# A two-stage attention kernel: the MLP of the first stage computed by rows with folded weights, started inside the attention loop

## Chip, cores and metric

The kernel runs on one core of one Trainium2 chip. The metric is the device time in microseconds (us) of one execution; the median over several executions is compared. Engines are named TensorE (PE in the rows), VectorE (DVE), ScalarE (ACT), GpSimd (POOL) and SyncE (SP).

## The reference

Four images of 16 x 16 pixels and 128 channels pass two layers. Cut to what matters here:

```
# layer 0: attention with 8 heads over 64 sampled points, residual, MLP, residual
x_ln = layernorm(x, ln_g, ln_b)
q = x_ln @ wq + bq                 # -> depthwise conv, gelu, offsets -> sampled keys and values
att = softmax(qh @ kh.T) @ vh      # 8 heads of 16 channels
z = att @ mo_w + mo_b + x
out = gelu(layernorm(z, ln_g, ln_b) @ mlp_w + mlp_b) + z          # called x1 below
# layer 1: group norm (32 groups, over pixels and 4 channels), full attention, residual
xg = groupnorm(x1) * gn_gamma + gn_beta
q, k, v = xg @ wq + bq, xg @ wk + bk, xg @ wv + bv
y = softmax(q @ k.T / sqrt(C)) @ v @ wo + bo + x1
```

## The kernel before

Everything stays on chip after the loads. Each engine has its own program, written out by hand, with semaphores between them; nothing schedules it. Where an instruction waits, all that stands behind it on its engine waits too. "bank" is one of eight PSUM banks of 512 fp32 columns; only TensorE writes them, and VectorE and ScalarE read them. GpSimd reads and writes SBUF only.

The stages:
- Until about 24 us: loads, layer norm of x, convolution, sampling, keys of the first two images.
- The loop of the first attention (lines 1048 to 1063 of TensorE's program), over T = 8 tiles of 128 pixels (two per image). Step i transposes the shifted scores of tile i (transpose_scores), multiplies with the values for tile i-1 (value_tile), projects tile i-2 (out_project), makes the scores of tile i+2 (score_tile) and transposes the normalised result of tile i-1 (att_transpose). VectorE takes maxima, subtracts, normalises and adds the residual (z_tile), ScalarE takes exponentials and copies. At i = 2, fold_second (line 914) makes the folded weight w_vo = wv wo and three bias columns in bank 7; ScalarE's fold_out (line 411) copies them out.
- The bridge, from the loop to the second attention. Per image b: bn_stats and bn_aggr of z (z_stats, z_aggr), the variance plus eps (z_var), its power -1/2 on GpSimd (z_scale, line 314), z_hat = (z - mean) * rstd on VectorE (zhat_image, line 648), transposes of z and z_hat to channels x pixels (z_transpose, line 1002), ScalarE's copy of the latter into z_t (zt_image), one matmul of 256 columns with mlp_wg = ln_g * mlp_w (mlp_image, line 1020), Gelu with a bias column (gelu_image), and the sum with the transposed z (x1_image, line 653) in transposed layout x1_t. gelu_transpose turns gel_t back to rows for the residual of layer 1, which VectorE adds to z_res (x1_residual, line 658); z_res = z + out_bias comes from GpSimd (residual, line 319). The output bias in out_bias is made by three matmuls after z_transpose(0) (lines 1174 to 1178).
- Group norm in two sets of two images: gn_stats, gn_aggr; gn_mean (line 1071) multiplies the means with a matrix that leaves each channel's deviation from its group; gn_square (line 700) squares it on VectorE, gn_spread (line 1083) sums the variances, gn_var adds eps, gn_pow on GpSimd takes the power -1/2, and norm_image (line 712) writes x_gn. keep_warm (line 812) issues bf16 matmuls on a bank nobody reads; three pairs stand in the bridge (lines 1190 to 1196).
- The second attention, from gn_mean(1) at line 1208: project_qk, project_v, score_image, transposes and value products per image, and finish_tile (line 731), which writes y with the residual x1_res.

VectorE's order in the bridge stands in lines 746 to 805, ScalarE's in lines 448 to 476, GpSimd's in lines 332 to 345, TensorE's in lines 1172 to 1228.

Of the kernel before, what the change touches and what calls it, by code (L numbers as in the profile page):

```python
# [37 lines left out]
def reach(shift, n):  # L38
# [10 lines left out]
              ("mk_b", 1), ("mv_b", 1), ("gn_gamma", 1), ("gn_beta", 1), ("bq1", 1), ("bk1", 1), ("bv1", 1), ("mlp_b", 1),  # L49
# [3 lines left out]
    "late": [("mlp_w", C), ("wv1T", C), ("wo1", C), ("wq1", C), ("wk1", C), ("group_mean", P), ("group_rest", P)],  # L53
}
ROWS = ["bq_conv", "ln_b", "mo_b", "bo1"]
# [13 lines left out]
def build(nc, x, early, fold, mid, late, rows, ln_rows, out):  # L69
    ctx = ExitStack()  # L70
    with ctx:
# [27 lines left out]
        def r(name):  # L99
# [17 lines left out]
        cols1 = sb("cols1", [P, 3])  # L117
# [3 lines left out]
        mlp_wg = sb("mlp_wg", [P, C])  # L121
        msa_bias = sb("msa_bias", [P, C])
# [30 lines left out]
        z_hat = sb("z_hat", [P, T, C])  # L153
        z_t = sb("z_t", [P, T, P])
        gel_t = sb("gel_t", [P, B, HW])
# [26 lines left out]
                fold1_mm w_vo_ok cols1_ok outbias_mm outbias_ok msabias_mm msabias_ok mlpw_ok gamma_ok""",  # L182
# [4 lines left out]
            "norm of z and MLP": "zst_ok zmv_ok zve_ok zrs_ok zhat_ok zt_mm zt_ok mlp_mm gel_ok zres_ok x1t_ok gelt_mm x1res_ok",  # L187
# [80 lines left out]
        def _(pool):  # L268
# [50 lines left out]
            def residual(b):  # L319

                pool.wait_ge(s["z_ok"], 2 * b + 2)
                pool.wait_ge(s["outbias_ok"], 1)
                pool.tensor_tensor(z_res[:, 2 * b:2 * b + 2, :], z[:, 2 * b:2 * b + 2, :],
                                   out_bias[:, :].unsqueeze(1).to_broadcast([P, S, C]), ALU.add).then_inc(s["zres_ok"], 1)
# [10 lines left out]
            pool.wait_ge(s["w_vo_ok"], 1)  # L335
            pool.tensor_scalar(w_vog[:, :], w_vo[:, :], w("gn_gamma"), None, ALU.mult).then_inc(s["gamma_ok"], 1)
            z_scale(1)
            residual(0)
            residual(1)
# [3 lines left out]
            residual(2)  # L343
            residual(3)
            gn_pow(1)

        @block.scalar
        def _(act):
# [61 lines left out]

            def fold_out():
                act.wait_ge(s["fold1_mm"], 1)
                act.copy(w_vo[:, :], bank[7][:, 0:C]).then_inc(s["w_vo_ok"], 1)
                for j, name in enumerate(("bq1", "bk1", "mlp_b")):
                    act.activation(cols1[:, j:j + 1], bank[7][:, C + j:C + j + 1], ACT.Identity, bias=w(name)).then_inc(s["cols1_ok"], 1)
# [28 lines left out]
            def gelu_image(b):  # L444
                act.wait_ge(s["mlp_mm"], b + 1)
                act.activation(gel_t[:, b], bank[3 + b][:, 0:HW], ACT.Gelu, bias=cols1[:, 2:3]).then_inc(s["gel_ok"], 1)

            for i in range(T - 1):
# [61 lines left out]
        def _(dve):  # L510
# [156 lines left out]
            for i in range(T - 1):  # L667
# [21 lines left out]
                if i >= 5 and i % 2 == 1:  # L689
                    zhat_image((i - 5) // 2)  # L690
# [602 lines left out]
```

## Time and profile before

| | us |
|---|---|
| median of 3 runs | 79.36 (79.25 to 79.98) |
| the profiled execution's own time | 79.27 |
| its span in the trace | 77.40 |
| TensorE matmuls busy | 70.6 (91% of the span) |
| VectorE busy | 51.7 (67%) |
| ScalarE busy | 33.9 (44%) |
| GpSimd busy | 24.3 (31%) |

The span is what the trace shows from the first to the last instruction; the 1.87 us around it are start and end of the execution. A row of a timeline gives start, duration, engine, line and operation, then output<-inputs, the shapes and how many instructions are merged ("x2"). In square brackets stands the idle time of the engine before the row and who ended it. An fp32 matmul is recorded as two instructions, a transpose as one. A matmul's duration includes its latency: in a row of several, the next starts long before the last has ended, so the time that one takes from the queue is read from start to start.

### The profile page before, as it was taken

To read this page: it belongs to the slowest core of one execution; us is meant where nothing else is said; L and a number is where in the kernel's file an instruction comes from. 1 tells how busy PE (TensorE), PEld (TensorE's weight loads), DVE (VectorE), ACT (ScalarE), POOL (GpSimd) and SP (SyncE) were. 2 spreads that over 40 slices of the span, in tenths; PEclk is the share of its full clock that TensorE was granted. 3 is DMA by queue.
4 is the path that set the end of the run, shared out by engine and by line. 5 is a ranking of instruction groups with operands and counts; after the bars stand their busy time and mean duration, and the time that the engine had idled before them with its cause. 6 is when DMAs were issued, how large, how long until landed. Compare 5 with 4: busy or idle time off the path is not lost.

```text
span 77.4 us, 1968 instructions
## 1 busy us (share of the span) xinstructions
PE 70.6 (91%) x732; PEld 53.6 (69%) x732; DVE 51.7 (67%) x172; ACT 33.9 (44%) x84; POOL 24.3 (31%) x37
## 2 busy tenths in 40 slices
PE   4999699998999999999999999998897999998950
PEld 2345599783786647879777989845485869996830
DVE  0478742116366959477789968599799786868480
ACT  6112397068139563524424419820248048263600
POOL 5008999900000038390019137123820030000000
PEclk9999999999999999999999999999999999999999
DMA  0789870000000000000000000000000000010112
GB/s 9 226 270 150 305 289 12 0 8 0 0 8 0 0 0 4 0 0 8 0 0 0 4 0 0 8 0 0 0 0 0 0 0 4 0 68 9 59 55 89
DMA packets 3051, 3.07 MB, mean 40 GB/s; under 512 B 225, under 2 KB 2657, under 8 KB 3042
## 3 DMA queue, kind: packets, MB, share of 16 engines
q1 hardware_dynamic: 3042, 2.95, 12.8%
q8 instruction: 6, 0.10, 0.5%
q14 instruction: 3, 0.02, 0.1%
HBM read 2.42 MB, written 0.52 MB: 38 GB/s over the span
## 4 chain that ended last, share of the span: by engine, by line
PE 63%; DVE 17%; issue 5%; DMA 5%; ACT 3%; SPq 2%; POOL 2%; DVEq 0%; POOLq 0%; ACTq 0%
PE bank L810 53%; DMA x_hw<-x 5%; PE bank L971 5%; PE bank L1140 2%; DVE smax L604 2%; DVE x_t L656 1%; DVE gst L694 1%; SPq L247 1%; DVE st L528 1%; DVE bilin L578 1%; DVE x_gn L716 1%; DVE dist_y L562 1%; PE bank L989 1%; DVE q_conv L517 1%; POOL grs L330 1%
## 5 line engine op out<-in xcount | busy, mean ns | idle before, releaser
L810 PE MATMUL bank<-k_blk,qh 128*128 128x512 f32 x16 | 8.4, 605 | 0.0
L810 PE MATMUL bank<-v_blk,p_t 128*128 128x34 f32 x64 | 7.8, 267 | 0.0
L810 PEld LDWEIGHTS bank<-v_blk,p_t 128*128 128x128 f32 x64 | 7.8, 192 | 0.0
L810 PE MATMUL bank<-warm 128*128 128x512 bf16 x18 | 6.3, 471 | 1.0 <-POOL warm L269 1.0
L604 DVE TENSOR_REDUCE smax<-bank 128x8 f32<-128x512 f32 x8 | 5.5, 685 | 2.4 <-PE bank L810 2.4
L317 POOL TENSOR_TENSOR zrs<-zve,neg_half 128x2 f32<-128x2 f32 x4 | 2.9, 714 | 12.7 <-DVE zve L646 12.7
L810 PE MATMUL bank<-q_ph,wd 128*32 128x112 f32 (+5 forms) x256 | 6.8, 249 | 0.0
L303 POOL TENSOR_TENSOR x_res<-x_st,msa_bias 128x1024 f32<-128x1024 f32 x1 | 2.4, 2358 | 12.8 <-DVE bilin L578 12.8
L431 ACT ACTIVATE p_t<-bank 128x512 f32<-128x512 f32 x8 | 4.8, 597 | 3.4 <-PE bank L971 3.4
L810 PEld LDWEIGHTS bank<-q_ph,wd 128*32 128x32 f32 x256 | 5.6, 109 | 0.7 <-issue 0.3
L611 DVE TENSOR_TENSOR s_sub<-bank,smax 128x512 f32<-128x512 f32 x8 | 5.5, 682 | 0.1
L280 POOL TENSOR_TENSOR wd<-pack_early 128x512 f32<-128x512 f32 x4 | 4.1, 1046 | 4.4 <-DVE x_hat L540 4.4
L810 PE MATMUL bank<-v,p_t 128*128 128x129 f32 x32 | 4.8, 284 | 0.6 <-ACT p_t L233 0.4
L810 PEld LDWEIGHTS bank<-v,p_t 128*128 128x128 f32 x32 | 4.2, 190 | 1.2 <-issue 1.0
L971 PE MATMUL bank<-pack_early,s_sub 128*128 128x128 f32 x32 | 5.0, 279 | 0.0
L488 ACT ACTIVATE p<-bank,nmax 128x256 f32<-128x256 f32 x8 | 3.4, 476 | 3.0 <-DVE nmax L728 2.8
L438 ACT COPY att_t<-bank 128x128 f32<-128x128 f32 x8 | 2.1, 263 | 5.4 <-PE bank L989 5.3
L971 PEld LDWEIGHTS bank<-pack_early,s_sub 128*128 128x128 f32 x32 | 3.7, 144 | 0.8 <-issue 0.5
L810 PE MATMUL bank<-k,q 128*128 128x256 f32 x16 | 4.2, 385 | 0.0
L528 DVE BATCH_NORM_STATS2 st<-x_hw 128x6 f32<-128x128 f32 x8 | 1.8, 283 | 3.2 <-DMA x_hw<-x 3.2
L810 PEld LDWEIGHTS bank<-warm 128*128 128x128 bf16 x18 | 2.0, 122 | 2.9 <-issue 1.9
L810 PE MATMUL bank<-pack_mid,att_t 128*128 128x128 f32 x16 | 3.7, 311 | 0.2 <-DVE z L634 0.2
(149 smaller groups left out, 161.2 us busy)
## 6 DMA issues: line engine op xcount, KB each, us to landing
x_st<-x SPq DMA_DIRECT2D x1, 512.0 KB, 6.7
pack_late<-late SPq DMA_DIRECT2D x1, 448.0 KB, 7.3
out<-y SPq DMA_DIRECT2D x3, 128.0 KB, 1.7
pack_fold<-fold SPq DMA_DIRECT2D x1, 320.0 KB, 4.1
pack_mid<-mid SPq DMA_DIRECT2D x1, 261.0 KB, 5.8
x_hw<-x SPq DMA_DIRECT2D x2, 128.0 KB, 2.2
x_hw<-x SPq DMA_DIRECT2D x1, 256.0 KB, 3.8
pack_early<-early SPq DMA_DIRECT2D x1, 184.0 KB, 2.5
```

What stands on the lines that cost most here:

```text
L280: pool.tensor_tensor(wd[:, n:n + WD_CHUNK].rearrange("p n k j -> p (n k) j"), w("ident32").unsqueeze(1).to_broadcast([P, WD_CHUNK * PHASES ...
L303: pool.tensor_tensor(x_res[:, :, :], x_st[:, :, :].rearrange("p b (s c) -> p (b s) c", s=S), msa_bias[:, :].unsqueeze(1).to_broadcast([P, ...
L317: pool.tensor_tensor(zrs[:, 2 * b:2 * b + 2], zve[:, 2 * b:2 * b + 2], neg_half[:, 0:2], ALU.pow).then_inc(s["zrs_ok"], 1)
L431: act.activation(p_t[:, i % 2].rearrange("p j q -> p (j q)"), bank[5 + i % 2][:, :], ACT.Exp).then_inc(s["exp_ok"], 1)
L438: act.copy(att_t[:, i % 2], bank[0][:, 0:P]).then_inc(s["attt_ok"], 1)
L488: act.activation(p1[:, b % 2, t], bank[5 + b % 2][:, t * HW:(t + 1) * HW], ACT.Exp, bias=nmax1[:, 2 * b + t:2 * b + t + 1]).then_inc(s["p1 ...
L528: dve.bn_stats(st[:, i], x_hw[:, i]).then_inc(s["stats"], 1)
L604: dve.tensor_reduce(smax[:, i % 2], scores(i), AX.X, ALU.max).then_inc(s["smax_ok"], 1)
L611: dve.tensor_tensor(s_sub[:, i % 2], scores(i), smax[:, i % 2].unsqueeze(2).to_broadcast([P, NH, PIX]), ALU.subtract).then_inc(s["ssub_ok" ...
L810: return pe.matmul(o, l, r_, start=start, stop=stop, **k)
L971: m = pe.transpose(bank[5 + i % 2][:, j * P:(j + 1) * P], s_sub[:, i % 2, 2 * j:2 * j + 2].rearrange("p h q -> p (h q)"), w("ident"))
L1140: m = pe.transpose(bank[(2, 0)[t]][:, j * P:(j + 1) * P], p1[:, b % 2, t, j * P:(j + 1) * P], w("ident"))
```

## The change

1. The mean is taken out of the MLP's weights. A new constant center = I - 1/128 is loaded (in the pack "late"), and fold_mlp multiplies it with mlp_wg: z @ (center mlp_wg) is (z - mean) @ mlp_wg. The same function makes ln_b @ mlp_w + mlp_b as a full 128 x 128 block of equal rows. ScalarE copies both to mlp_wc (mlp_out).
2. The MLP works on rows: mlp_image multiplies z_t (now the transpose of z itself) as the stationary operand with mlp_wc, two matmuls of 128 columns into the upper half of zt_bank(b). VectorE's scaled_image multiplies with rstd and adds the bias block (u, two instructions per image); ScalarE's Gelu reads u from SBUF without a bias; gelu_transpose transposes gel into zt_bank(b), and x1_image adds z_t to it. z_hat, its transposes and zhat_image are gone.
3. x1_res = gel + z_res is added on GpSimd inside residual; x1_residual is gone from VectorE. GpSimd does residual(0) after the x_gn of images 0 and 1, and residual(1) to residual(3) after the last x_gn, behind gn_pow(1). The product w_vog moves behind gn_pow(0).
4. At i = 2 of the loop fold_mlp stands where fold_second stood. z_transpose(0) and zt_image(0) move into the loop (i = 5). mlp_image(0) and z_transpose(1) come right behind the loop. fold_second and the output bias (output_bias) move behind out_project(7) and mlp_image(3), into bank 6.
5. gn_square(0) runs on ScalarE as one Square; gn_square(1) stays on VectorE.
6. The three pairs of warm-up matmuls in the bridge are gone. Bank and semaphore waits follow the new places.

The diff, cut to its core:

```diff
-    "late": [("mlp_w", C), ("wv1T", C), ("wo1", C), ("wq1", C), ("wk1", C), ("group_mean", P), ("group_rest", P)],
+    "late": [("mlp_w", C), ("wv1T", C), ("wo1", C), ("wq1", C), ("wk1", C), ("group_mean", P), ("group_rest", P), ("center", P)],
...
 def residual(b):
+    t = slice(2 * b, 2 * b + 2)
     pool.wait_ge(s["z_ok"], 2 * b + 2)
     pool.wait_ge(s["outbias_ok"], 1)
...
+    pool.wait_ge(s["zres_ok"], b + 1)
+    pool.wait_ge(s["gel_ok"], b + 1)
+    pool.tensor_tensor(x1_res[:, t], gel[:, t], z_res[:, t], ALU.add).then_inc(s["x1res_ok"], 1)
...
             z_scale(1)
-            residual(0)
-            residual(1)
             z_scale(2)
             z_scale(3)
             gn_pow(0)
-            residual(2)
-            residual(3)
+            pool.wait_ge(s["w_vo_ok"], 1)
+            pool.tensor_scalar(w_vog[:, :], w_vo[:, :], w("gn_gamma"), None, ALU.mult).then_inc(s["gamma_ok"], 1)
+
+            pool.wait_ge(s["xgn_ok"], 2)
+            residual(0)
             gn_pow(1)
+
+            pool.wait_ge(s["xgn_ok"], B)
+            for b in range(1, B):
+                residual(b)
...
+            def mlp_out():
+                act.wait_ge(s["foldm_mm"], 1)
+                act.copy(mlp_wc[:, :], bank[7][:, 0:2 * C]).then_inc(s["mlpf_ok"], 1)
...
             def gelu_image(b):
-                act.wait_ge(s["mlp_mm"], b + 1)
-                act.activation(gel_t[:, b], bank[3 + b][:, 0:HW], ACT.Gelu, bias=cols1[:, 2:3]).then_inc(s["gel_ok"], 1)
+                t = slice(2 * b, 2 * b + 2)
+                act.wait_ge(s["u_ok"], 2 * b + 2)
+                act.activation(gel[:, t], u[:, t], ACT.Gelu).then_inc(s["gel_ok"], 1)
...
             att_tile(T - 1)
-            zt_image(2)
+            gn_square(0)
             gelu_image(2)
+            fold_out()
             zt_image(3)
+            act.wait_ge(s["outbias_mm"], 1)
+            act.copy(out_bias[:, :], bank[6][:, HW:HW + C]).then_inc(s["outbias_ok"], 1)
             gelu_image(3)
...
-            def zhat_image(b):
+            def scaled_image(b):
+                dve.wait_ge(s["mlp_mm"], b + 1)
                 dve.wait_ge(s["zrs_ok"], b + 1)
-                for i in (2 * b, 2 * b + 1):
-                    dve.tensor_scalar(z_hat[:, i], z[:, i], zmv[:, i, 0:1], zrs[:, i:i + 1], ALU.subtract, ALU.mult).then_inc(s["zhat_ok"], 1)
+                dve.wait_ge(s["mlpf_ok"], 1)
+                for t in range(S):
+                    i = 2 * b + t
+                    dve.scalar_tensor_tensor(out=u[:, i], in0=zt_bank(b)[:, HW + t * C:HW + (t + 1) * C], scalar=zrs[:, i:i + 1], in1=mlp_wc[:, C:2 * C],
+                                             op0=ALU.mult, op1=ALU.add).then_inc(s["u_ok"], 1)
...
-                dve.wait_ge(s["gel_ok"], b + 1)
-                dve.tensor_tensor(x1_t[:, b], gel_t[:, b], zt_bank(b)[:, HW:2 * HW], ALU.add).then_inc(s["x1t_ok"], 1)
...
                 dve.wait_ge(s["gelt_mm"], b + 1)
-                dve.wait_ge(s["zres_ok"], b + 1)
-                dve.tensor_tensor(x1_res[:, 2 * b:2 * b + 2], bank[3 + b][:, HW:2 * HW].rearrange("p (s c) -> p s c", s=S),
-                                  z_res[:, 2 * b:2 * b + 2], ALU.add).then_inc(s["x1res_ok"], 1)
+                dve.tensor_tensor(x1_t[:, b], zt_bank(b)[:, 0:HW], z_t[:, 2 * b:2 * b + 2, :].rearrange("c s q -> c (s q)"), ALU.add).then_inc(s["x1t_ok"], 1)
...
+            def fold_mlp():
+
+                pe.wait_ge(s["mlpw_ok"], 1)
+                pe.wait_ge(s["qh_ok"], 2)
+                mm(bank[7][:, 0:C], w("center"), mlp_wg[:, :])
+                mm(bank[7][:, C:2 * C], w("ln_b").to_broadcast([P, P]), w("mlp_w"), stop=False)
+                mm(bank[7][:, C:2 * C], ones_row[:, :], r("mlp_b"), start=False).then_inc(s["foldm_mm"], 1)
...
+            def output_bias():
+                pe.wait_ge(s["w_vo_ok"], 1)
+                pe.wait_ge(s["cols1_ok"], 2)
+                o = bank[6][:, HW:HW + C]
+                mm(o, w("bv1").to_broadcast([P, P]), w("wo1"), stop=False)
+                mm(o, w("gn_beta").to_broadcast([P, P]), w_vo[:, :], start=False, stop=False)
+                mm(o, ones_row[:, :], r("bo1"), start=False).then_inc(s["outbias_mm"], 1)
...
                 if i == 2:
-                    fold_second()
+                    fold_mlp()
+                if i == T - 3:
+                    z_transpose(0)
+
+            mlp_image(0)
+            z_transpose(1)
```

VectorE's queue around the group norm of images 0 and 1 stood before as follows (gve and gmean are the statistics of gn_var, x_res is x1_res, x_t is x1_t):

```order
L709 TENSOR_SCALAR gve<-bank 128x2 [waits gvar_mm]
L710 COPY gmean<-bank 128x2
L651 TENSOR_SCALAR z_hat<-z,zmv,zrs 128x128 [waits zrs_ok]
L651 TENSOR_SCALAR z_hat<-z,zmv,zrs 128x128
L716 TENSOR_SCALAR x_gn<-x_t,gmean,grs 128x256 [waits grs_ok,gmean_ok] x2
L661 TENSOR_TENSOR x_res<-bank,z_res 128x256 [waits zres_ok,gelt_mm]
L656 TENSOR_TENSOR x_t<-gel_t,bank 128x256 [waits gel_ok]
L694 BN_STATS gst<-x_t 128x6 [waits x1t_ok]
L722 TENSOR_SCALAR q<-bank,cols 128x256 [waits cols1_ok,qk_mm]
L723 TENSOR_SCALAR k<-bank,cols 128x256
```

And now (u is the scaled MLP output of image 3, x_t that of image 2):

```order
L725 TENSOR_SCALAR gve<-bank 128x2 [waits gvar_mm]
L726 COPY gmean<-bank 128x2
L679 TENSOR_TENSOR x_t<-bank,z_t 128x256 [waits gelt_mm]
L709 BN_STATS gst<-x_t 128x6 [waits x1t_ok]
L673 SCALAR_TENSOR_TENSOR u<-bank,zrs,mlp_wc 128x128 [waits mlpf_ok,zrs_ok,mlp_mm]
L673 SCALAR_TENSOR_TENSOR u<-bank,zrs,mlp_wc 128x128
L732 TENSOR_SCALAR x_gn<-x_t,gmean,grs 128x256 [waits grs_ok,gmean_ok] x2
L738 TENSOR_SCALAR q<-bank,cols 128x256 [waits cols1_ok,qk_mm]
L739 TENSOR_SCALAR k<-bank,cols 128x256
```

The x1 of image 2, its statistics and the two scaled rows of image 3 stand ahead of the x_gn pair, where two z_hat stood; x1 of image 2 waits for gelt_mm, a transpose by TensorE.

TensorE's queue from the group norm's second step to the first projection stood before as follows:

```order
L810 MATMUL bank<-gmv,pack_late 128x2 [waits dev2_ok]
L810 MATMUL bank<-dev,pack_late 128x2
L810 MATMUL bank<-gmv,pack_late 128x2
L1014 MATMUL bank<-pack_early,z 128x128 [waits x1t_ok,z_ok]
L1014 MATMUL bank<-pack_early,z 128x128
L1017 MATMUL bank<-pack_early,z_hat 128x128 [waits zhat_ok]
L1017 MATMUL bank<-pack_early,z_hat 128x128
L1014 MATMUL bank<-pack_early,z 128x128 [waits x1t_ok,z_ok]
L1014 MATMUL bank<-pack_early,z 128x128
L1017 MATMUL bank<-pack_early,z_hat 128x128 [waits zhat_ok]
L1017 MATMUL bank<-pack_early,z_hat 128x128
L810 MATMUL bank<-z_t,mlp_wg 128x256 [waits att_ok,mlpw_ok,zt_ok]
L810 MATMUL bank<-x_gn,wq1g 128x256 [waits x1res_ok,gamma_ok,xgn_ok]
L810 MATMUL bank<-x_gn,wk1g 128x256
```

And now, with the output bias (rows with w_vo and row) inside:

```order
L821 MATMUL bank<-gmv,pack_late 128x2 [waits dev2_ok]
L821 MATMUL bank<-dev,pack_late 128x2
L821 MATMUL bank<-gmv,pack_late 128x2
L821 MATMUL bank<-mlp_wc,z_t 128x128 [waits mlpf_ok,zt_ok]
L821 MATMUL bank<-mlp_wc,z_t 128x128
L821 MATMUL bank<-pack_late,pack_early 128x128 [waits cols1_ok,w_vo_ok]
L821 MATMUL bank<-w_vo,pack_early 128x128
L821 MATMUL bank<-row,ones_row 128x128
L1093 MATMUL bank<-pack_early,gel 128x128 [waits u_ok,gel_ok]
L1093 MATMUL bank<-pack_early,gel 128x128
L821 MATMUL bank<-x_gn,wq1g 128x256 [waits ssub_ok,gamma_ok,xgn_ok]
L821 MATMUL bank<-x_gn,wk1g 128x256
```

The transpose of gel of image 2 that x1 waits for now stands behind the MLP of image 3 and the output bias, and ahead of the projection.

ScalarE's queue ahead of the copy that the MLP of image 3 needs (the second z_t below; the cols rows are the two bias columns of layer 1) stood before:

```order
L438 COPY att_t<-bank 128x128 [waits msa_mm,attt_mm]
L442 COPY z_t<-bank 128x256 [waits zt_mm]
L446 ACTIVATE gel_t<-bank,cols 128x256 [waits mlp_mm]
L442 COPY z_t<-bank 128x256 [waits zt_mm]
L446 ACTIVATE gel_t<-bank,cols 128x256 [waits mlp_mm]
```

And now:

```order
L453 COPY z_t<-bank 128x256 [waits zt_mm]
L449 COPY att_t<-bank 128x128 [waits msa_mm,attt_mm]
L463 ACTIVATE dev<-bank 128x2 [waits dev_mm]
L458 ACTIVATE gel<-u 128x256 [waits u_ok]
L424 COPY w_vo<-bank 128x128 [waits fold1_mm]
L426 ACTIVATE cols<-bank,pack_early 128x1 x2
L453 COPY z_t<-bank 128x256 [waits zt_mm]
```

The square, the Gelu of image 2 and the copies of w_vo and two columns stand between the two z_t copies now.

## Rows read from the trace of the kernel before

**Rows 1.** TensorE's timeline, loop of the first attention and just behind it: start, duration, instruction.
```profile
34.53 0.39 PE L810 MATMUL bank<-pack_late 128*128 128x128 f32 x2
...
35.34 0.63 PE L971 MATMUL bank<-pack_early,s_sub 128*128 128x128 f32 x4
...
42.94 0.60 PE L971 MATMUL bank<-pack_early,s_sub 128*128 128x128 f32 x4
...
44.49 0.38 PE L1014 MATMUL bank<-pack_early,z 128*128 128x128 f32 x2
44.71 0.38 PE L1017 MATMUL bank<-pack_early,z_hat 128*128 128x128 f32 x2
44.93 0.39 PE L810 MATMUL bank<-pack_late,pack_early 128*128 128x128 f32 x2
...
45.89 0.66 PE L971 MATMUL bank<-pack_early,s_sub 128*128 128x128 f32 x4
```

**Rows 2.** TensorE's timeline, 52 to 61 us.
```profile
52.32 0.38 PE L810 MATMUL bank<-gmv,pack_late 128*128 128x2 f32 x2
...
56.15 0.70 PE L810 MATMUL bank<-x_gn,wq1g 128*128 128x256 f32 x2 [0.26 <-DVE x_gn L716]
...
57.12 0.59 PE L810 MATMUL bank<-z_t,mlp_wg 128*128 128x256 f32 x2
57.55 0.38 PE L1068 MATMUL bank<-pack_early,gel_t 128*128 128x128 f32 x2
...
60.12 0.38 PE L810 MATMUL bank<-gmv,pack_late 128*128 128x2 f32 x2 [0.54 <-DVE gmv L698]
```

**Rows 3.** VectorE's timeline, 49 to 67 us.
```profile
49.40 0.29 DVE L626 TENSOR_TENSOR att<-bank,recip 128x128 f32<-128x128 f32 x1
...
50.30 0.42 DVE L656 TENSOR_TENSOR x_t<-gel_t,bank 128x256 f32<-128x256 f32 x1 [0.32 <-ACT gel_t L446]
...
52.02 0.24 DVE L698 BATCH_NORM_AGGREGATE gmv<-gst 128x2 f32<-128x6 f32 x2
...
55.36 1.46 DVE L716 TENSOR_SCALAR x_gn<-x_t,gmean,grs 128x256 f32<-128x256 f32 x2 [0.40 <-POOL grs L330]
...
57.87 0.47 DVE L722 TENSOR_SCALAR q<-bank,cols 128x256 f32<-128x256 f32 x1
...
58.97 0.41 DVE L656 TENSOR_TENSOR x_t<-gel_t,bank 128x256 f32<-128x256 f32 x1
...
59.76 0.30 DVE L698 BATCH_NORM_AGGREGATE gmv<-gst 128x2 f32<-128x6 f32 x2
...
63.12 0.73 DVE L716 TENSOR_SCALAR x_gn<-x_t,gmean,grs 128x256 f32<-128x256 f32 x2 [0.22 <-POOL grs L330]
...
66.33 0.35 DVE L738 SCALAR_TENSOR_TENSOR y<-bank,rec,x_res 128x128 f32<-128x128 f32 x1
```

**Rows 4.** GpSimd's timeline, 34 to 57 us.
```profile
34.14 0.61 POOL L312 TENSOR_SCALAR mlp_wg<-pack_late,pack_early 128x128 f32<-128x128 f32 x1
...
54.47 0.79 POOL L330 TENSOR_TENSOR grs<-gve,neg_half 128x2 f32<-128x2 f32 x1 [0.61 <-DVE gve L709]
55.22 1.45 POOL L323 TENSOR_TENSOR z_res<-z,out_bias 128x256 f32<-128x256 f32 x2
```

**Rows 5.** ScalarE's timeline, 36 to 55 us.
```profile
36.65 0.58 ACT L415 ACTIVATE cols<-bank,pack_early 128x1 f32<-128x1 f32 x3
...
47.63 1.28 ACT L466 ACT_TABLE_LOAD   x1
...
49.80 0.85 ACT L446 ACTIVATE gel_t<-bank,cols 128x256 f32<-128x256 f32 x2 [0.23 <-PE bank L810]
...
54.72 0.37 ACT L442 COPY z_t<-bank 128x256 f32<-128x256 f32 x1 [3.92 <-PE bank L1017]
```

**Rows 6.** The page, part 2: granted clock of TensorE in 40 equal slices, in tenths.
```profile
PEclk9999999999999999999999999999999999999999
```

**Rows 7.** The chain that ended last, in order of time: start, duration, work.
```profile
64.26 3.07 PE bank L810 x20
```

More of the change, by code:

```diff
@@ L186, in build @@
             "attention": """s_mm smax_ok ssub_ok pt_mm exp_ok av_mm recip_ok att_ok attt_mm attt_ok msa_mm xres_ok z_ok""",
-            "norm of z and MLP": "zst_ok zmv_ok zve_ok zrs_ok zhat_ok zt_mm zt_ok mlp_mm gel_ok zres_ok x1t_ok gelt_mm x1res_ok",
+            "norm of z and MLP": "zst_ok zmv_ok zve_ok zrs_ok zt_mm zt_ok mlp_mm u_ok gel_ok zres_ok gelt_mm x1t_ok x1res_ok",
             "group norm": "gst_ok gmv_ok dev_mm dev2_ok gvar_mm gve_ok gmean_ok grs_ok xgn_ok",
@@ L786, in _ @@
             gn_aggr(3)
-            x1_residual(3)
             gn_square(1)
@@ L1013, in z_transpose @@
                 for t in range(S):
-                    pe.transpose(zt_bank(b)[:, HW + t * P:HW + (t + 1) * P], z[:, 2 * b + t], w("ident"))
-                pe.wait_ge(s["zhat_ok"], 2 * b + 2)
-                for t in range(S):
-                    m = pe.transpose(zt_bank(b)[:, t * P:(t + 1) * P], z_hat[:, 2 * b + t], w("ident"))
+                    m = pe.transpose(zt_bank(b)[:, t * P:(t + 1) * P], z[:, 2 * b + t], w("ident"))
                 m.then_inc(s["zt_mm"], 1)
@@ L1021, in mlp_image @@
                 pe.wait_ge(s["zt_ok"], b + 1)
-                pe.wait_ge(s["mlpw_ok"], 1)
-                if b < 2:
-                    pe.wait_ge(s["ssub_ok"], T - 1 + b)
-                else:
-                    pe.wait_ge(s["att_ok"], T)
-                mm(bank[3 + b][:, 0:HW], mlp_wg[:, :], z_t[:, 2 * b:2 * b + 2, :].rearrange("c s q -> c (s q)")).then_inc(s["mlp_mm"], 1)
+                pe.wait_ge(s["mlpf_ok"], 1)
+                for t in range(S):
+                    m = mm(zt_bank(b)[:, HW + t * C:HW + (t + 1) * C], z_t[:, 2 * b + t], mlp_wc[:, 0:C])
+                m.then_inc(s["mlp_mm"], 1)
             N = len(SHIFTS)
@@ L1181, in _ @@
             value_tile(T - 2)
+            mlp_image(1)
             out_project(T - 3)
-            z_transpose(1)
             value_tile(T - 1)
             att_transpose(T - 2)
-            mlp_image(0)
-            mlp_image(1)
-            out_project(T - 2)
-            att_transpose(T - 1)
-            keep_warm(2, 6)
-            out_project(T - 1)
             gelu_transpose(0)
             gelu_transpose(1)
-            keep_warm(2, 6)
+            out_project(T - 2)
+            z_transpose(2)
+            att_transpose(T - 1)
+            mlp_image(2)
+            out_project(T - 1)
+            fold_second()
             gn_mean(0)
-            keep_warm(2, 6)
+            z_transpose(3)
             gn_spread(0)
-            z_transpose(2)
-            z_transpose(3)
-            mlp_image(2)
+            mlp_image(3)
+            output_bias()
+            gelu_transpose(2)
             project_qk(0)
-            mlp_image(3)
-            gelu_transpose(2)
+            gelu_transpose(3)
             project_v(0)
-            gelu_transpose(3)
             project_qk(1)
```

109 lines of the change are left out of this document (51 added, 58 removed).

## The prediction, made before the changed kernel had run

> **What bounds the kernel now.** I read the chain of waits first, then the timelines of the four engines between 34 and 64 us, because every edit lies there. Three stretches matter. In the loop of the first attention TensorE never waits: its rows follow each other without idle time from the folded weights at 34.53 to the last out-projection of the loop, whose successor starts at 44.49 [rows 1]. From there to 60.12 the kernel hops between engines (transpose, copy, Gelu, transpose, add, statistics, group norm), and what counts is the order in which each queue meets its waits. TensorE's idle time before 60.12 (0.54 us, released by VectorE's gmv) shows where this bridge ends [rows 2]. From 60.12 on, the second attention runs mostly on TensorE, and the change leaves its order as it was. So I take the start of gn_mean(1), 60.12, as the marker: what moves it moves the end. Readers should see in the rows of VectorE that from 55.36 to 60.06 that engine has almost no idle time [rows 3], while around 50 to 55 it shares the path with GpSimd and ScalarE.
>
> **The start and the loop.** The DMAs change by some columns: center adds 64 KB to a pack that GpSimd needs only at 34.14 [rows 4]. I count nothing.
> fold_mlp takes fold_second's place in TensorE's queue, but it reads mlp_wg, which GpSimd finishes at 34.14 + 0.61 = 34.75 [rows 4], while fold_second started at 34.53 [rows 1]. A wait costs some 0.06 more (gmv ends at 59.76 + 0.30 = 60.06, TensorE starts at 60.12 [rows 2, 3]), so the fold starts at 34.81: +0.28. Queued behind it are the score transposes of every later tile. The old fold took 35.34 - 34.53 = 0.81. The new one is three matmuls like those of the output bias before, 45.89 - 44.93 = 0.96 [rows 1]: +0.15. As TensorE does not wait until 44.49, all of this persists. The two transposes of z, now inside the loop, add 44.71 - 44.49 = 0.22 [rows 1]. The loop ends at 44.49 + 0.28 + 0.15 + 0.22 = 45.14.
> After the loop four transposes and the output bias go (1.40 us up to 45.89). One MLP (57.55 - 57.12 = 0.43 [rows 2]) and two transposes (0.22) come: 45.79. So tile 7 is transposed 0.1 earlier than before; the second MLP costs its 0.43 a little later.
>
> **What is gained by 52 us.** ScalarE copies z_t of image 0 in the loop and no longer ahead of the table load. The load starts one copy (0.37) and a little earlier, near 47.2 (now 47.63), and takes 1.28; the Gelus run from about 48.55 to 49.4 (now from 49.80) [rows 5]. Transposing gel back takes 0.11 of pitch and 0.27 of latency, so the first comes back near 49.5. VectorE first normalises attention tile 7, now at 49.40 [rows 3]: ahead of that tile's matmuls an MLP of 0.43 has replaced four transposes of 0.44, and a statistic and an aggregate more stand ahead of its reciprocal on VectorE, so I take 49.54 for it, and 0.21 later, at 49.75 instead of 50.30, x1 of image 0 starts. It ends at 50.16, and gmv, with one z addition fewer on the way, ends near 51.6 instead of 52.02 + 0.24 = 52.26 [rows 3]. The six warm-up matmuls go; they filled waits, so they give nothing.
>
> **Where it is lost again.** gn_mean(0) stands behind z_transpose(2), mlp_image(2), out_project(7) and fold_second. z_transpose(2) waits for the first x1 (50.16, so it starts at 50.22): transposes land at 50.66, ScalarE's copy (0.37 [rows 5]) at 51.06, the MLP takes 0.50 (0.43 running, and some 0.07 for the start after a wait: two of 256 columns take 0.97 from 56.15), the out-projection 0.3 (three matmuls of that size take 0.96 [rows 1]), the fold about 0.22 + 2 x 0.20 = 0.62 (0.81 less one column of the old fold's three): gn_mean(0) starts at 52.55, and now at 52.32 [rows 2]. The 0.68 won on VectorE is thus gone. Squaring on ScalarE (0.20 from the matmul's end at 52.90, as three one-column activations take 0.58) instead of two VectorE operations, and then the same matmuls and the same power on GpSimd, gives the scale near 55.0 (now 54.47 + 0.79 = 55.26) [rows 4].
> But VectorE is not there to use it: between gn_var(0) and norm_image(0) now stand x1 of image 2, its statistics and scaled_image(3). x1 of image 2 waits for a transpose which TensorE issues behind mlp_image(3) and output_bias, and mlp_image(3) waits for ScalarE, where the fourth z_t copy stands behind square, Gelu 2, the w_vo copy and two bias columns. In numbers: 53.04 after the square, + 0.38 Gelu (two take 0.85), + 0.16 for the w_vo copy (bounds 0 and the 0.37 of a copy twice as wide; I take the middle), + 2 x 0.19 for the columns (three take 0.58), + 0.37 for the copy: 54.33 [rows 5]. TensorE: 54.39, mlp_image(3) 0.50, output_bias 0.96, two transposes 0.38 to their end: 56.23. VectorE: x1 and statistics 59.76 - 58.97 = 0.79, then two scaled rows. These read PSUM and SBUF as the y operation does, which takes 0.35; less 0.08 of overlap each, 0.54. Their bounds are 0.35 a piece and 0.21, half of the 0.42 that an addition of twice the columns takes; I take the row of the same form. x_gn starts at 57.6, instead of 55.36.
> Here the largest gain of the change is paid out: residual additions on GpSimd waited for x_gn. Now the pair x_gn takes 1.46 while GpSimd adds z_res (55.22, 1.45 long), and 0.73 at 63.12, where GpSimd is idle [rows 3, 4]. After the change GpSimd waits until the pair is done. The first x_gn ends at 58.0 and TensorE projects at 58.06, against 56.15: +1.91.
>
> **What is won back.** The projection ends 0.97 + 0.16 later, 59.19, so q1 starts at 59.2 against 57.87 (VectorE was busy with a residual, x1 and statistics until then): +1.33. The residual between k1 and x1 of image 3 is gone (1.10 from q1 to x1 now, 0.78 after): x1 starts at 59.98 against 58.97. Statistics and gmv follow as before, and gn_mean(1) starts near 61.1 against 60.12: +0.97 [rows 2, 3].
> The second attention then starts from the same state. GpSimd's residuals of images 1 to 3, 1.45 each after the last x_gn (63.85 + 0.97), end near 66.3, 67.7 and 69.2, before the y rows of their images need them (the first of all is at 66.33 now, and image 0 is ready early). They cost nothing; gn_pow(1) stands before them.
> The sum is 79.27 us (the profiled execution; its span is 77.40) + 0.97 = 80.24. It lies 0.09 below the median of the runs shown, 79.36, for the same kernel. I predict 80.2.
> One term can be read otherwise. The new Gelu has neither bias column nor PSUM source; the nearest row has both, two in 0.85, which is 0.38 to the next start and 0.47 for one [rows 5], and the sum uses that.
> The Trainium skill (ScalarE: Activation LUTs, What ACT_TABLE_LOAD costs) gives 186 ns + 0.833 ns per column without such a column operand, 0.40 for 256. By it one Gelu on the path is 0.07 shorter and the time would be 80.17. No row here shows that form of Gelu.
>
> **Rivals.**
> *The clock falls (82.0).* TensorE loses its warm-up matmuls and gets a hole of 2 us at 56 to 58, beside some 2 us of smaller waits from 49 on. Against it: the granted clock is 9 tenths or more in every slice of the profile now, those of the start included [rows 6]. For it: the longest wait of TensorE in this stretch is 0.54 us now [rows 2]. If the clock goes to 1.2 GHz, matmuls take double: a stretch such as 64.26 to 67.33, 3.07 us of TensorE [rows 7], would take 3 more; with part hidden by waits I price 1 to 3 over my sum: 81.2 to 83.2.
> The Trainium skill (TensorE: Matmul & The Clock Gate, What's actually happening) says that the slow clock is the default and activity releases it. By that rule a quiet bridge can be punished after it, not in it; the trace, at full clock throughout, neither shows nor excludes it.
> *The loop has cover (79.5).* If the fold's wait and longer matmuls are absorbed (VectorE or ScalarE late anyway in that iteration) and the ScalarE queue before the fourth copy is shorter, 0.43 and 0.2 to 0.3 go from the sum.
> *VectorE is released early (faster, 77.8 to 78.5).* One condition decides: the transpose of gel of image 2 must land by 53.7, so that x1, statistics and the scaled rows (0.79 + 0.54) lie under the wait for the rsqrt. Then x_gn starts at 55.0, its pair costs 0.73 instead of 1.46, q1 starts at 56.6, and gn_mean(1) near 58.6: -1.5. By my sum the transpose lands at 56.23, 2.5 us too late. Half of the way would give about no change.
> *GpSimd blocks VectorE in the second attention (80.9).* If operations from PSUM suffer as x_gn did, one projection output behind each of the additions from 64.8 to 69.2 loses up to 0.7. Against it: a projection output reads PSUM, while x_gn reads SBUF alone; no row shows one beside GpSimd.
>
> **How the numbers follow.** My sum 55% (79.8 to 80.6 by its term sizes); loop covered 17%; clock 11%; released or half released 12%; GpSimd blocking 5%. The range 79.0 to 81.6 leaves out the released case and the upper clock case. More than 1% (0.8 us, about what a measurement of this kernel can tell from no change) slower means over 80.15: slightly over half of my case, the clock, the blocking: 0.50. Faster 0.11. Within 1%: 0.39.
>
> **What would show it.** Right: TensorE's first fold row at about 34.8; x1 of image 0 near 49.8; VectorE idle for nearly 2 us after gmean, released by TensorE; x_gn as a pair of 0.73; a TensorE hole of 2 us before the projection; 61.1 for gn_mean(1). Wrong: x_gn starting before 56, a granted clock below 9 anywhere, or VectorE rows longer than now between 64 and 69 us.

## The result and the profile after

The changed kernel takes 81.94 us (81.47 to 83.04, 4 executions), the kernel before 79.31 beside it: ratio 1.029 [1.024, 1.035]. The forecast was 80.2, with a range of 79.0 to 81.6. The direction is right, the size is not: the rival "the clock falls" is what happens in most executions. The mean granted clock of TensorE was 1.000 in the execution of 81.47, and 0.974, 0.956 and 0.958 in those of 81.66, 82.23 and 83.04. Ratios here and below compare only the executions of each kernel that lie within 1.5% of its fastest; medians and ranges are of all of them.

Two things have to be taken apart before the profiles can be compared. First the start. The profiled execution of after (81.47, its span 79.7) ran late before any changed work. TensorE's timeline of after:

```profile
4.70 0.59 PE L821 MATMUL bank<-pack_early,ones_col 128*1 128x128 f32 x2
5.22 1.03 PE L821 MATMUL bank<-warm 128*128 128x512 bf16 x2
6.04 1.05 PE L821 MATMUL bank<-pack_early,x_hat 128*128 128x128 f32 x6
```

and of before:

```profile
4.68 0.60 PE L810 MATMUL bank<-warm 128*128 128x512 bf16 x2
5.21 1.00 PE L810 MATMUL bank<-pack_early,x_hat 128*128 128x128 f32 x6
```

Two warm-up matmuls take 1.03 instead of 0.60: full speed comes later here. In the clock records of the traces it sets in 6.48 us after the start in after and 3.81 in before (the page shows 9 for the time ahead of it too). The first score transpose starts at 27.73 instead of 26.65: 1.08 late. That differs from execution to execution: over the traces below it starts at 26.61 to 27.27 in kernels made from before, at 26.31 to 27.73 in those made from after. The two ranges overlap, so the late start is not put down to the change. I take 1.08 off every time of after below ("net").

Second the bridge. TensorE's timeline of after, from the fold in the loop to gn_mean(1):

```profile
35.87 0.49 PE L821 MATMUL bank<-mlp_wg,pack_late 128*128 128x128 f32 x2
...
36.93 0.66 PE L997 MATMUL bank<-pack_early,s_sub 128*128 128x128 f32 x4
...
46.78 0.38 PE L1040 MATMUL bank<-pack_early,z 128*128 128x128 f32 x2
47.17 0.63 PE L997 MATMUL bank<-pack_early,s_sub 128*128 128x128 f32 x4
...
50.47 0.74 PE L1093 MATMUL bank<-pack_early,gel 128*128 128x128 f32 x4
...
53.99 0.36 PE L821 MATMUL bank<-gmv,pack_late 128*128 128x2 f32 x2
...
55.65 0.71 PE L821 MATMUL bank<-mlp_wc,z_t 128*128 128x128 f32 x4 [0.21 <-ACT z_t L453]
56.20 0.39 PE L821 MATMUL bank<-pack_late,pack_early 128*128 128x128 f32 x2
...
57.15 0.44 PE L1093 MATMUL bank<-pack_early,gel 128*128 128x128 f32 x2
59.40 0.70 PE L821 MATMUL bank<-x_gn,wq1g 128*128 128x256 f32 x2 [1.81 <-DVE x_gn L732]
...
62.51 0.38 PE L821 MATMUL bank<-gmv,pack_late 128*128 128x2 f32 x2 [0.45 <-DVE gmv L713]
```

VectorE's timeline of after:

```profile
46.75 0.28 DVE L645 TENSOR_TENSOR att<-bank,recip 128x128 f32<-128x128 f32 x1
...
49.29 0.61 DVE L673 SCALAR_TENSOR_TENSOR u<-bank,zrs,mlp_wc 128x128 f32<-128x128 f32 x2
...
50.75 0.20 DVE L638 RECIPROCAL recip<-bank 128x8 f32<-128x8 f32 x1
50.99 0.29 DVE L645 TENSOR_TENSOR att<-bank,recip 128x128 f32<-128x128 f32 x1
51.20 0.75 DVE L679 TENSOR_TENSOR x_t<-bank,z_t 128x256 f32<-128x256 f32 x2
...
55.55 0.15 DVE L726 COPY gmean<-bank 128x2 f32<-128x2 f32 x1
57.63 0.42 DVE L679 TENSOR_TENSOR x_t<-bank,z_t 128x256 f32<-128x256 f32 x1 [1.92 <-PE bank L1093]
58.08 0.43 DVE L709 BATCH_NORM_STATS2 gst<-x_t 128x6 f32<-128x256 f32 x1
58.43 0.59 DVE L673 SCALAR_TENSOR_TENSOR u<-bank,zrs,mlp_wc 128x128 f32<-128x128 f32 x2
58.94 0.72 DVE L732 TENSOR_SCALAR x_gn<-x_t,gmean,grs 128x256 f32<-128x256 f32 x2
```

ScalarE's timeline of after:

```profile
50.02 0.71 ACT L458 ACTIVATE gel<-u 128x256 f32<-128x256 f32 x2
...
55.20 0.39 ACT L453 COPY z_t<-bank 128x256 f32<-128x256 f32 x1
```

and GpSimd's:

```profile
55.73 0.69 POOL L334 TENSOR_TENSOR grs<-gve,neg_half 128x2 f32<-128x2 f32 x1
```

The scale grs ends at 56.42 and nobody uses it until 58.94. VectorE stands for 1.92 us with x1 of image 2 at its head; the transpose it waits for is TensorE's row at 57.15, behind the MLP of image 3 and the output bias. Then TensorE stands for 1.81. Marker by marker (each is the start of the work named), net of the start:

| marker | before | after, net | moved | predicted |
|---|---|---|---|---|
| score transposes of tile 3 | 35.34 | 35.85 | +0.51 | +0.43 |
| those of tile 7 | 45.89 | 46.09 | +0.20 | -0.10 |
| gn_mean(0) | 52.32 | 52.91 | +0.59 | +0.23 |
| x_gn of image 0 | 55.36 | 57.86 | +2.50 | +2.24 |
| first projection | 56.15 | 58.32 | +2.17 | +1.91 |
| gn_mean(1) | 60.12 | 61.43 | +1.31 | +0.97 |

The last y moves +1.21 net (77.38 against 75.09). So at full clock and with the same start the change costs 1.2 us; the sum said 0.97. What is missing up to the median is in the main the clock, as the next run shows.

### The profile page after: what moved, and what is told of

Read it like the earlier page. It is cut to its first block, busy times and chain, and to the rows that moved or that the text cites. A ratio compares the mean times of both kernels' runs of the same rounds, so it can differ in the third digit from the quotient of the medians.

```text
span 79.7 us, 1971 instructions
## 1 busy us (share of the span) xinstructions
PE 70.9 (89%) x730; PEld 53.8 (68%) x730; DVE 49.6 (62%) x166; ACT 33.6 (42%) x85; POOL 27.1 (34%) x41
## 4 chain that ended last, share of the span: by engine, by line
PE 71%; DVE 14%; ACT 5%; issue 4%; POOL 4%; DVEq 0%; POOLq 0%
PE bank L821 62%; PE bank L997 4%; POOL k_blk L309 3%; PE bank L1168 2%; DVE smax L623 2%; DVE x_t L679 1%; DVE q_conv L536 1%; DVE bilin L597 1%; PE bank L1040 1%; DVE dist_y L581 1%; DVE u L673 1%; DVE s_sub L630 1%; ACT z_t L453 1%; POOL mlp_wg L313 1%; PE bank L1015 1%
## 5 line engine op out<-in xcount | busy, mean ns | idle before, releaser
L821 PE MATMUL bank<-warm 128*128 128x512 bf16 x12 | 5.2, 587 | 1.0 <-POOL warm L270 1.0
L325 POOL TENSOR_TENSOR z_res<-z,out_bias 128x256 f32<-128x256 f32 x4 | 2.9, 724 | 3.7 <-DVE x_gn L732 3.7
L821 PE MATMUL bank<-x_gn,wq1g 128*128 128x256 f32 x8 | 2.5, 392 | 1.8 <-DVE x_gn L732 1.8
```

Of the source, the lines that this page charges most:

```text
L325: pool.tensor_tensor(z_res[:, t], z[:, t], out_bias[:, :].unsqueeze(1).to_broadcast([P, S, C]), ALU.add).then_inc(s["zres_ok"], 1)
L821: return pe.matmul(o, l, r_, start=start, stop=stop, **k)
```

## The experiments

**again2: the changed kernel unchanged; pad2: one zero column more in the early pack.**

> The changed kernel once more, unchanged. In its first profile 1.08 us of the 2.3 us were lost before 28 us, where the program is almost the same: the slow matmuls lasted until 6.5 us instead of 3.8 and the first pack landed 0.3 us later. Theory A (chance of the start): the profile of this run has its start nearer to that of the kernel before (first attention transposes of tile 0 at 26.7 to 27.2), and the times scatter over 1 us. Theory B (the change causes it): they are at 27.6 to 27.9 again. Theory C (the clock falls in the bridge, as the mean clocks of 0.96 to 0.97 of three of the four executions may say): a profile with a mean clock under 1.00 shows rows at half speed between 50 and 65 us, and its time is 82 or more.

> The changed kernel with one column of zeros added to the pack early, so that its rows are 360 columns (1440 bytes) long again instead of 359 (1436). Theory B1 (rows of odd length load slower and shift the start): the pack lands at 4.25 us instead of 4.55, q_conv starts at 7.5 instead of 8.3, and the time falls by 0.8 to 1.1 us to about 80.8. Theory A (chance of the start): no difference from the changed kernel beyond its own scatter.

```diff
-              ("ident32", BLK), ("ident", P), ("wq_conv", C)],
+              ("ident32", BLK), ("ident", P), ("wq_conv", C), ("pad", 1)],
```

Both medians are 82.69, ratios 1.034 [1.025, 1.043] and 1.037 [1.030, 1.045]: the row length of the pack makes no difference that these runs show, and in pad2 q_conv starts at 8.00, not at 7.5. The start of again2 was that of before (26.69), and it shows what sets the median. Its stretches (length, busy us and count for TensorE, its weight loads, VectorE, ScalarE and GpSimd, then TensorE's granted clock, DMA share and GB/s):

```profile
50.00:55.94 5.94, 5.06 (x39) 4.28 (x37) 3.79 (x18) 1.75 (x8) 2.48 (x4) 1.00 0.01 3
55.94:62.77 6.83, 5.02 (x17) 3.73 (x17) 3.85 (x12) 1.32 (x4) 1.49 (x3) 0.50 0.00 0
62.77:72.00 9.23, 9.22 (x61) 8.10 (x60) 6.18 (x18) 5.26 (x13) 4.99 (x7) 1.00 0.04 15
```

Granted is half of the clock, 1.2 GHz, from 55.94 to 62.77. Its projection on TensorE's timeline:

```profile
58.72 1.22 PE L821 MATMUL bank<-x_gn,wq1g 128*128 128x256 f32 x2 [1.81 <-DVE x_gn L732]
59.74 1.06 PE L821 MATMUL bank<-x_gn,wk1g 128*128 128x256 f32 x2
```

From start to start 1.02 instead of 0.53 in after. gn_mean(1) starts at 63.19: +3.07 against before, where after has +1.31 net. The last y is at 77.96, +2.83 without the 0.04 of its start, against +1.21: the fall costs 1.6 us. The execution profiled for after is the only one of the fourteen of after, again2 and pad2 without it: the mean granted clock of the other thirteen is 0.955 to 0.977.

**warm2: six warm-up matmuls ahead of the first projection.**

> The changed kernel with six warm-up matmuls on a free bank in TensorE's hole before the first projection of the second attention. Theory C (without warm-up work the clock falls in or after the bridge in some executions): mean clock back to 1.00 in all of them, slowest execution near the fastest, median 0.3 to 0.8 us lower. Theory D (the bridge's queue order alone): same median within 0.2 us and the same scatter.

```diff
             gelu_transpose(2)
+            keep_warm(6, 3)
 
             project_qk(0)
```

80.88 us (80.61 to 83.1), ratio 1.019 [1.013, 1.026], clock full in the profile. TensorE's wait before the projection is filled and the projection starts no later (58.70, where again2 had 58.72). The gain over again2, 1.81 us, is over twice the 0.3 to 0.8 expected, and the clock is not back in all executions: its mean was 0.958 in the one that took 83.1 and 0.979 in that of 81.39, and 0.993 or more in the other three.

**pairs: three pairs put back, at places that correspond to those of before; both: pairs and warm2 together.**

> The changed kernel with the three warm-up pairs put back at the places that correspond to those of before (behind mlp_image(2), gn_mean(0) and gn_spread(0), into bank 3), not at the wait of 1.8 us. By theory A (the pairs hold the clock) the clock is full in most executions: median 80.5 to 81.3, at 0.1 to 0.4 us more than the undisturbed path of 81.0 at most. By theory B (the wait before the projection decides) it falls as in the unchanged changed kernel: 82.3 to 83.

> The changed kernel with both sets of warm-up matmuls: the pairs of the run pairs and the six before the first projection of the run warm2. Either set alone left the time at 1.019 and 1.023 of before, the unchanged changed kernel is at 1.034. If the clock's fall depends on all of TensorE's idle time from 50 to 59 us, both together hold it: 80.6 to 81.1 us, ratio 1.015 to 1.02, few executions over 81.5. If the sets do nothing and the runs only scattered, the executions spread from 80.7 to 83 as there.

```diff
             att_transpose(T - 1)
             mlp_image(2)
+            keep_warm(2, 3)
             out_project(T - 1)
             fold_second()
             gn_mean(0)
+            keep_warm(2, 3)
             z_transpose(3)
             gn_spread(0)
+            keep_warm(2, 3)
             mlp_image(3)
```

pairs: 81.50 us (80.92 to 82.65), ratio 1.023 [1.018, 1.028], a little over the 80.5 to 81.3 expected. Five of the six executions ran with a mean clock of 1.000. Its profiled execution, the slowest, is the sixth (0.972) and shows the fall, later and half as long:

```profile
50.00:59.25 9.25, 7.03 (x50) 5.51 (x49) 5.89 (x28) 2.53 (x13) 2.66 (x4) 1.00 0.01 2
59.25:62.66 3.41, 3.11 (x10) 2.63 (x11) 1.57 (x5) 0.38 (x1) 1.45 (x2) 0.50 0.00 0
```

both: 81.10 us, 80.71 to 81.25 over all six executions, ratio 1.019 [1.015, 1.024], as expected, and no mean clock under 0.999. Either set alone left executions in which the time goes up to 82.65 or 83.1; both together left none over 81.25. The filler matmuls have a price of their own: in both the first projection starts 2.73 behind that of before, net of its start, where after has 2.17, and the last y +1.92 behind, where after has +1.21.

**cool and cool2: the kernel before without its three pairs.**

> The kernel before without its three warm-up pairs of matmuls between 50 and 53 us; the output is the same. Theory A (the pairs hold TensorE's clock, and their removal is why the changed kernel falls to 1.2 GHz from about 56 us in most executions): the clock falls here too, in most executions, and the median is 80.5 to 82. Theory B (the fall comes of the changed order, above all the wait of 1.8 us before the first projection; the pairs only fill waits): the clock stays full and the median is that of the kernel before, 79.2 to 79.6, within 0.3%.

> The kernel cool once more (before without its three warm-up pairs), for a second profile: its 12 times went from 79.13 to 81.78 and the profile was taken of the fastest. If the slower executions are clock falls, a profile of one over 80 us shows a stretch at half of the clock (1.2 GHz) after 50 us, and one under 79.6 shows none.

```diff
             att_transpose(T - 1)
-            keep_warm(2, 6)
             out_project(T - 1)
             gelu_transpose(0)
             gelu_transpose(1)
-            keep_warm(2, 6)
             gn_mean(0)
-            keep_warm(2, 6)
             gn_spread(0)
```

cool: 80.46 us (79.13 to 81.78, 12 executions), at the lower edge of theory A's 80.5 to 82, ratio 1.008 [1.003, 1.012]. The profile was taken of the fastest execution, and there all markers up to gn_mean(1) stand within 0.05 of before, at full clock; the removed matmuls had filled waits and nothing else moved. But in ten of its twelve executions the mean granted clock was 0.957 or 0.978; the two others (0.996 and 0.998) are the fastest. cool2 caught an execution of 79.85, between the two times that its expectation spoke of, and it shows the fall: its page's line of the granted clock first, then the stretches:

```profile
PEclk9999999999999999999999999999569999999999
```

```profile
50.00:54.45 4.45, 2.83 (x20) 2.25 (x20) 4.06 (x21) 1.01 (x3) 1.43 (x2) 1.00 0.02 4
54.45:57.86 3.41, 3.41 (x14) 3.12 (x14) 2.67 (x9) 0.90 (x3) 2.21 (x3) 0.50 0.00 0
```

The mean granted clock of each execution completes the picture. It is either 0.979 or less, or 0.993 or more. Where an execution of the first kind was profiled (again2, pad2, pairs, cool2), it has a stretch at half clock that begins in the bridge:

| kernel | executions | of these with 0.979 or less |
|---|---|---|
| before, run beside the others | 43 | 0 |
| cool, cool2 | 13 | 11 |
| after, again2, pad2 | 14 | 13 |
| warm2 | 5 | 2 |
| pairs | 6 | 1 |
| both | 6 | 0 |
| guard | 6 | 0 |
| xgnfirst2 | 11 | 5 |
| best | 6 | 2 |
| bestwarm | 6 | 0 |

So the pairs did hold the clock of the kernel before, whose order has no long wait at all: theory A is right. Theory B's medians (79.2 to 79.6) did not come. The kernel before loses 0.8% without its pairs by the ratio, and 1.3% by the medians of all executions (80.46 against 79.43). In the changed kernel the fall costs 1.6 us in again2, 2% of its time. Its bridge also leaves TensorE more idle time. The stretch from 50 to 59 us, TensorE's busy time behind the length, in after:

```profile
50.00:59.00 9.00, 6.67 (x47) 5.24 (x46) 6.06 (x29) 2.89 (x13) 2.62 (x4) 1.00 0.01 2
```

and in before:

```profile
50.00:59.00 9.00, 8.24 (x51) 5.87 (x50) 8.15 (x31) 2.95 (x9) 3.63 (x5) 1.00 0.00 0
```

That the wait of 1.81 alone does not decide is shown by cool, which has no such wait, and by pairs, which keeps it and loses the clock in one of six executions. That idle time as a whole decides is not shown: no run varied it in steps, and best, with TensorE busy for 8.31 of these 9 us, has two executions of lower mean clock.

**guard: the kernel before, GpSimd's additions of images 2 and 3 behind the first x_gn pair.**

> The kernel before, with one more wait: GpSimd adds z_res of images 2 and 3 only after the first x_gn pair. Theory (VectorE's x_gn pair took 1.46 us because GpSimd added beside it): the pair takes 0.73, the first projection starts 0.35 earlier (near 55.8), q1 and what follows up to 0.7 earlier, and the time is 78.6 to 79.0. Rival (the pair was slow for another reason, or the additions only slow what comes next, the residual and x1 of image 2): 79.2 to 79.6.

```diff
             gn_pow(0)
+            pool.wait_ge(s["xgn_ok"], 2)
             residual(2)
             residual(3)
```

78.64 us (78.28 to 79.07), ratio 0.990 [0.986, 0.994]: as expected, faster than before by one more line. VectorE's timeline of guard, and below it GpSimd's:

```profile
55.99 0.74 DVE L717 TENSOR_SCALAR x_gn<-x_t,gmean,grs 128x256 f32<-128x256 f32 x2 [0.40 <-POOL grs L330]
56.63 0.42 DVE L662 TENSOR_TENSOR x_res<-bank,z_res 128x256 f32<-128x256 f32 x1
57.06 0.42 DVE L657 TENSOR_TENSOR x_t<-gel_t,bank 128x256 f32<-128x256 f32 x1
```

```profile
56.80 1.42 POOL L323 TENSOR_TENSOR z_res<-z,out_bias 128x256 f32<-128x256 f32 x2 [0.92 <-DVE x_gn L717]
```

The pair takes 0.74, against 1.46 in [rows 3]. GpSimd now adds from 56.80 to 58.22 beside VectorE's next operations, which read PSUM, and these take 0.42 as ever (0.41 before): only the operation with both its tensors in SBUF was slowed. The Trainium skill (SBUF — State Buffer, Who interferes with whom) says that where VectorE and GpSimd need the shared ports the one that issues later is fully blocked, and that a VectorE instruction with at most one SBUF input outside the faster modes does not contend. The two traces agree: in before GpSimd started first (55.22 against 55.36) and only VectorE got slower, and the operations with one SBUF input kept their 0.42.

**xgnfirst2: the x_gn pair ahead of x1, statistics and scaled rows on VectorE.**

> The changed kernel with the two x_gn of images 0 and 1 moved ahead of x1, statistics and scaled rows of images 2 and 3 in VectorE's queue. My theory (VectorE is held by a transpose that comes late, and pays it at the projection): x_gn starts when the scale is there, near 56.5 instead of 58.9, the first projection follows output_bias near 57.6 instead of 59.4, and gn_mean(1) comes 0.5 to 1.2 us earlier; time 0.5 to 1.2 lower. Rival (the same work only changes places, since VectorE has to do x1, statistics and the scaled rows before gn_mean(1) in any case): gain below 0.3 us.

```diff
             gn_var(0)
+            norm_image(0)
+            norm_image(1)
             x1_image(2)
             gn_stats(2)
             scaled_image(3)
-            norm_image(0)
-            norm_image(1)
             project_out(0)
```

79.51 us (79.13 to 81.6, 11 executions), ratio 1.000 [0.996, 1.004]. The two lines give back all that the change had cost, and far more than the 0.5 to 1.2 us expected. In the profiled executions, both at full clock, the last y comes 1.3 us earlier than in after (74.98 against 76.30, each net of its start). The rest of the gain fits the clock, which fell in five of eleven executions here. VectorE's timeline:

```profile
55.78 0.73 DVE L732 TENSOR_SCALAR x_gn<-x_t,gmean,grs 128x256 f32<-128x256 f32 x2 [0.82 <-POOL grs L334]
```

x_gn follows GpSimd's power directly, and TensorE projects at 56.69, right behind the transpose of gel at 56.41. Now output_bias and that transpose are what is late.

**best: the queues reordered throughout; bestwarm: the same with five warm-up matmuls, two ahead of mlp_image(2), two ahead of mlp_image(3) and one ahead of the first projection.**

> The changed kernel with its queues reordered: fold_mlp one iteration later (takes 0.26 of wait away), x_gn of images 0 and 1 ahead of x1, statistics and scaled rows, gn_mean(0) ahead of the second fold, the square and power of the group norm ahead of the last row norm's, output_bias and fold_out off the way to the first projection. If the queue order is what cost the time: first projection near 55.0 in the trace, gn_mean(1) near 59, and 77.2 to 78.0 us, faster than both kernels, with the clock full. If the clock falls even so, 78.5 to 79.5. If the form of the change itself (longer chain per image) sets the time, no better than the kernel before: 79.2 to 79.6.

> best with five warm-up matmuls put into TensorE's waits: two before mlp_image(2), two before mlp_image(3), one before the first projection, all into bank 3. The median of best, 78.17, lies 0.9 above its fastest execution, 77.24. If that spread is TensorE's clock lost in the bridge, the median here is 77.3 to 77.7. If it is the start (at what time the clock rises at first) or anything else, 78.0 to 78.4, as best.

```diff
-                if i == 2:
+                if i == 3:
                     fold_mlp()
...
-            fold_second()
             gn_mean(0)
-            z_transpose(3)
+            fold_second()
             gn_spread(0)
+            z_transpose(3)
+            gelu_transpose(2)
             mlp_image(3)
-            output_bias()
-            gelu_transpose(2)
-
             project_qk(0)
-            gelu_transpose(3)
-            project_v(0)
             project_qk(1)
+            gelu_transpose(3)
+            output_bias()
+            project_v(0)
             gn_mean(1)
```

Beside that, ScalarE's copy of the folded weights (mlp_out) comes one iteration later, VectorE runs gn_var(0) ahead of the last aggregates and x_gn, then scaled_image(3), ahead of x1 of image 2; GpSimd runs gn_pow(0) ahead of z_scale(3); ScalarE runs fold_out behind the fourth z_t copy and the out_bias copy last; project_qk no longer waits for w_vog, project_v does. TensorE's timeline of best:

```profile
36.61 0.27 PE L1015 MATMUL bank<-pack_early,att 128*128 128x128 f32 x1
36.72 0.39 PE L821 MATMUL bank<-mlp_wg,pack_late 128*128 128x128 f32 x2
...
53.36 0.38 PE L1093 MATMUL bank<-pack_early,gel 128*128 128x128 f32 x2
...
54.78 0.70 PE L821 MATMUL bank<-x_gn,wq1g 128*128 128x256 f32 x2
...
58.34 0.28 PE L821 MATMUL bank<-gmv,pack_late 128*128 128x2 f32 x2
```

The fold waits for nothing any more. best takes 78.17 us (77.24 to 79.22), ratio 0.978 [0.972, 0.984]; bestwarm 77.84 (77.62 to 78.39), ratio 0.981 [0.977, 0.986]. Both beat before and the changed kernel. best is slightly over the 77.2 to 78.0 expected, and bestwarm lies between its two forecasts (77.3 to 77.7 and 78.0 to 78.4), so the medians don't decide between them. The spread shrinks from 1.98 to 0.77 us, by the slow end: 79.22 to 78.39. The two slowest executions of best, 78.56 and 79.22, had a mean granted clock of 0.978, the mean of cool2 with its 3.41 us at half clock; the four others of best and all six of bestwarm had 1.000. So best's slow end is a loss of clock as well; where in the kernel it fell is not on record. That the fillers cost anything here is not shown: the profiled executions' times are 0.58 apart, and 0.52 of it is there at the first score transpose.

## Why the prediction was right or wrong

- *The start, counted at nothing:* right; what the profiles differ by there is scatter.
- *fold_mlp +0.28 and +0.15:* right for the wait (0.26: 35.87 less 1.08 is 34.79, against 34.53 in [rows 1]). The fold itself takes 1.06 to the next transposes against 0.81 before, so +0.25. In best, where it waits for nothing, it takes 0.95, so the 0.96 of the sum was right for a fold without a wait. That the rows persist ("loop has cover") was right; that rival is false.
- *The loop's end, -0.1:* it is +0.20. Beside the fold's 0.1, the transposes of tile 7 start 0.39 behind z_transpose(1), where I took 0.22. They wait for the attention tile 5 (att_ok in transpose_scores), which VectorE ends at 46.75 + 0.28 = 47.03; TensorE starts at 47.17. The sum had no wait there.
- *x1 of image 0 at 49.75:* missed, 50.12 net. The term that was too small is the attention tile ahead of it, taken at 49.54: it started at 49.91 net. Gel's transposes start at 50.47, 49.39 net, and the first image is back near 49.8, later than "near 49.5" but still ahead of the attention tile. I had put only a statistic and an aggregate ahead of the reciprocal on VectorE. From 49.29 to 50.75 its queue is full with the scaled rows too. This 0.37 runs on to gn_mean(0) (52.91 instead of 52.55) and, hardly changed, to gn_mean(1) (61.43 instead of 61.1).
- *What the new Gelu costs:* 0.71 for two and 0.42 for one, where the sum used 0.47. The estimate by the formula of the Trainium skill (ScalarE: Activation LUTs, What ACT_TABLE_LOAD costs), 0.40, was the better value. It did not change the time noticeably.
- *ScalarE's queue ahead of the fourth copy, 54.33; the transposes of gel at 56.23:* 54.51 and 56.51 net, late by no more than x1 was. xgnfirst2 shows that this was the right place: taking x_gn out from behind that wait is worth 82.69 - 79.51 = 3.2 us in the median, the fall of the clock included, and 1.3 us at full clock.
- *The sum's own slips:* its terms give 52.48 for gn_mean(0), where it has 52.55, and 53.10 after the square, where it has 53.04; x1 of image 3 moves by 1.01, and the last marker is given 0.97. Together they are under 0.1 us and change nothing in the forecast.
- *The x_gn pair at 0.73 instead of 1.46:* right (0.72), and guard shows the reason.
- *"The six warm-up matmuls go; they filled waits, so they give nothing":* this is the step that failed. They did lie in waits (in cool nothing moves at full clock without them), but they were not worth nothing: they kept the clock. Without them it fell in 11 of 13 executions of the kernel before, with them in none of 43; in the changed kernel it fell in 13 of 14 without them and in one of six with them. I used the profile's full clock [rows 6] as evidence against a fall, though it was taken with the pairs in place, and gave the rival 11%. Its price was near: 1.6 in again2, where I had "1 to 3 over my sum". The sum with it, 79.27 + 0.97 + 1.6, is 81.8; measured were medians of 81.94 and 82.69.
- *VectorE released early:* false as the kernel stands, since the transposes land at 56.5 and not at 53.7. Its condition was met in best, with a different order of the queues: there they stand from 53.36 to 53.74, and its gn_mean(1) at 58.34 (58.68 if its start, 0.34 earlier than that of before, is put level) against the 58.6 that this rival named.
- *GpSimd blocks VectorE in the second attention:* false. In after, q of image 2 takes 0.48 beside GpSimd's additions, as it did before.

## What to carry to other kernels

An instruction that another engine waits for belongs ahead of work that itself waits: two lines moved on one queue were worth the whole loss. That filler matmuls lie in waits does not make them free to delete. Look at the mean granted clock of several executions without them, since one profile can show the full clock while most executions lose it. Before an operation with SBUF operands on VectorE is called slow, look at what GpSimd does at that time.

## What was not expected of the hardware

- The clock fell without a long wait. In cool2 the longest wait of TensorE between 50 and 54.45 us is 0.66 us, and it was busy 2.83 of 4.45 us; in again2 it was busy 5.06 of the 5.94 us ahead of the fall. In the same kernel one execution shows the fall and the next none (cool2 and cool), so what it costs in the median depends on the share of executions that have it.
- The stretch at half clock is not the wait, and it does not begin behind it: in again2 the fall at 55.94 comes 1.0 us before TensorE's work ahead of its wait ends (the transpose of gel, 56.23 + 0.69), and 4 us of the stretch lie on the matmuls behind the wait.
- Where GpSimd and VectorE met, VectorE alone paid: its pair of 0.74 became 1.46, while GpSimd's two additions took 1.45 as against 1.42 in guard.
